# A GNN convolution kernel: edge-range work of VectorE in 18 parts, GpSimd's tables at the head, read-back tables at half step 10

## What is computed

```python
h   = x @ W_in + b_in
Wij = (ssp(edge_attr @ Wf1 + bf1) @ Wf2 + bf2) * edge_weight[:, None]   # ssp = softplus - log 2
agg = segment_sum(h[dst] * Wij, src)
x   = layernorm(x + ssp(agg @ Wo1 + bo1) @ Wo2 + bo2)
# graph attention over the same edges:
e     = leaky_relu(h_att[src] @ a1 + h_att[dst] @ a2); e -= max(e)
alpha = exp(e) / (segment_sum(exp(e), dst)[dst] + 1e-9)
x   = layernorm(x + leaky_relu(x + neigh + (x * neigh) @ W2 + b2))
#   neigh = segment_sum((x @ W1 + b1)[src] * alpha, dst)
```

## Time and profile before

| | before |
|---|---|
| median of 3 runs | 1405.86 us (1402.91 to 1408.44) |
| the profiled execution, its own time | 1404.69 us |
| its span, first to last instruction | 1402.6 us |
| busy: PE, VectorE (DVE), ScalarE (ACT), GpSimd (POOL) | 83%, 86%, 61%, 59% |
| mean granted TensorE clock | 0.919 of full speed |

### The profile page before, as it was taken

One profiled execution on the slowest core, in us unless ns is written; L12 is line 12 of the kernel. 1 busy time (PEld: TensorE's weight loads), 2 busy tenths in 40 slices (PEclk: granted clock), 3 DMA queues, 4 the chain that ended last, 5 costly groups with the idle time before them and its releaser, 6 DMA issues. The chain is left out here.

```text
span 1402.6 us, 27868 instructions
## 1 busy us (share of the span) xinstructions
PE 1162.7 (83%) x8987; PEld 946.7 (67%) x9079; DVE 1204.6 (86%) x2226; ACT 853.5 (61%) x2125; POOL 831.4 (59%) x909
## 2 busy tenths in 40 slices
PE   4778767688899968899888999999999495777895
PEld 4444445357778756788767877777777384777895
DVE  8798866549899968799889999999998279999986
ACT  1456664478788978688888888888875044000023
POOL 5167777777777777777777777777777330000011
PEclk8688887899999999999999999999999798879998
DMA  7233342258899568899699999989897773776661
GB/s 263 68 81 91 89 115 79 74 124 215 222 263 255 190 194 225 240 251 258 179 244 263 242 244 260 264 230 241 246 265 203 178 245 104 241 226 222 230 226 37
DMA packets 246738, 276.49 MB, mean 197 GB/s; under 512 B 35121, under 2 KB 194511, under 8 KB 243252
## 3 DMA queue, kind: packets, MB, share of 16 engines
q1 hardware_dynamic: 200128, 185.24, 45.5%
q0 software_dynamic: 25856, 53.42, 12.2%
q10 hardware_dynamic: 20596, 35.89, 12.0%
HBM read 163.26 MB, written 111.20 MB: 196 GB/s over the span
## 5 line engine op out<-in xcount | busy, mean ns | idle before, releaser
L1929 POOL DMA_INDIRECT edge_rows<-x_rows,pos x808 | 783.5, 970 | 286.6 <-issue 225.8
L1441 ACT ACTIVATE h_edge<-ps_wh,w_col 128x128 f32<-128x128 f32 x808 | 229.4, 367 | 112.1 <-PE ps_wh L1232 99.7
L1276 PEld LDWEIGHTS ps_d<-back_one,back 128*128 128x128 f32 x1914 | 231.2, 192 | 59.4 <-issue 56.0
L1276 PE MATMUL ps_d<-back_one,back 128*128 128x128 f32 x1914 | 240.3, 278 | 4.3 <-DVE agg_t L1743 4.0
L1239 PE MATMUL ps_wh<-wf,filt 128*128 128x128 f32 x1616 | 237.5, 293 | 1.5 <-DVE filt L1545 1.4
L1225 PE MATMUL ps_v<-f_t,wf 128*128 128x512 f32 x400 | 223.1, 641 | 0.0
L1549 DVE TENSOR_TENSOR x_rows<-ps_wh,h_edge 128x512 f32<-128x512 f32 x202 | 138.0, 683 | 85.0 <-ACT h_edge L1441 37.9
L1239 PEld LDWEIGHTS ps_wh<-wf,filt 128*128 128x128 f32 x1616 | 208.0, 201 | 3.4 <-DVE filt L1545 3.4
L1065 PE MATMUL ps_wh<-yard 128*128 128x150 bf16 x1575 | 139.1, 234 | 59.7 <-DVE yard L1055 29.7
L2393 PE MATMUL ps_wh<-loan,yard 128*126 128x129 f32 x1250 | 155.2, 288 | 38.9 <-DVE yard L2643 30.8
L1065 PEld LDWEIGHTS ps_wh<-yard 128*128 128x128 bf16 x1575 | 110.0, 100 | 103.7 <-DVE yard L1055 73.1
(11 more groups left out here) (346 smaller groups left out, 1398.8 us busy)
## 6 DMA issues: line engine op xcount, KB each, us to landing
c_tab<-yard SPq DMA_DIRECT2D x25, 1575.0 KB
yard<-c_tab SPq DMA_DIRECT2D x25, 1575.0 KB, 6.6
dst_bc<-dst ACTq DMA_DIRECT2D x99, 252.0 KB
back<-edge_rows SPq DMA_DIRECT2D x42, 516.0 KB, 8.5
edge_rows<-x_rows,pos POOLq DMA_INDIRECT x808
back<-edge_rows SPq DMA_DIRECT2D x48, 258.0 KB, 5.0
m_tab<-yard SPq DMA_DIRECT2D x25, 393.8 KB
mask_room<-m_tab SPq DMA_DIRECT2D x5, 1968.8 KB, 12.4
```

Of the source, the lines that this page charges most:

```text
L1276: mm = nc.tensor.matmul(acc(c), back_rows(n)[:, k0 + t, 0:D], back_one[:, m % 2, o + t, :], start=t == 0, stop=t == k1 - k0 - 1, skip_grou ...
L1441: copy = nc.scalar.activation(h_edge[:, j, q, :], ps_wh[:, bank, 1, q * D:(q + 1) * D], ACT.Copy, scale=w_col[:, t(q)])
L1929: return pool.indirect_dma_start(table[s], bass.IndirectOffsetOnAxis(places_here, 0), rows, None)
```

## The change

It does three things. VectorE's edge ranges go from 9 parts to 18, one at each half step from 24 to 41, with TensorE's five parts at 28, 30, 33, 36 and 38; the operations are the same, some in another order, and the fourteen comparisons go in four parts of 4, 3, 4 and 3, the seven `picks` in parts of 2, 3 and 2. All that follows (pairs, counts) begins one half step later. GpSimd makes its constant tables before its first scatter, without waiting for anything, in the buffer `back_one`, which nobody uses before half step 50; one of the seven tables is dropped for an existing one (`ones3`). `rest_of_tables` moves from half step 4 to half step 10, where it stands behind the pieces of that half step.

```diff
-CS_HIGH, CS_LOW, CS_RUN, CS_UNDER, CS_BELOW, CS_PASSES = 9, 10, 11, 13, 14, 19
+CS_HIGH, CS_RUN, CS_UNDER, CS_BELOW, CS_PASSES = 8, 11, 16, 19, 25
...
+            tables = back_one[:, 0, :, :].rearrange("p k n -> p (k n)")
+            anti = tables[:, 0:P]
+            blk_i = tables[:, P:P + NK].bitcast(I32)
...
+            TABLES_AT = 10
             R_FROM = 24
-            P_FROM = R_FROM + 16
+            P_FROM = R_FROM + 17
...
+            RANGE_STEPS = 18
             def ranges_dve_at(k):
-                return {R_FROM: 0, R_FROM + 5: 1, R_FROM + 6: 2, R_FROM + 7: 3, R_FROM + 8: 4, R_FROM + 9: 5,
-                        R_FROM + 11: 6, R_FROM + 13: 7, R_FROM + 15: 8}.get(k)
+                return k - R_FROM if R_FROM <= k < R_FROM + RANGE_STEPS else None
             def ranges_pe_at(k):
-                return {R_FROM + 7: 0, R_FROM + 9: 1, R_FROM + 10: 2, R_FROM + 12: 3, R_FROM + 14: 4}.get(k)
+                return {R_FROM + 4: 0, R_FROM + 6: 1, R_FROM + 9: 2, R_FROM + 12: 3, R_FROM + 14: 4}.get(k)
...
+                    if r == 6:
+                        link(nc.vector.tensor_scalar(src7, work_i[:, 2, :, :], 255, 8, ALU.bitwise_and,
+                                                     ALU.logical_shift_left))
+                        dve.wait_ge(r7_made, 6)
                         nc.vector.tensor_copy(iota_lo, iota_f[:])
                         nc.vector.tensor_copy(iota_key, key_i)
                         nc.vector.tensor_copy(tid, tid_i)
                         nc.vector.tensor_copy(three, three_i)
-                        nc.vector.tensor_scalar(blk_first, blk_i, float(W), None, ALU.mult)
-                        nc.vector.tensor_scalar(blk_last, blk_i, float(W), float(W - 1), ALU.mult, ALU.add)
-                        nc.vector.tensor_scalar(blk_key, blk_i, 256.0, None, ALU.mult)
-                        nc.vector.tensor_scalar(work_i[:, 0, :, :], src7, 7, None, ALU.logical_shift_right)
...
-                        for c in range(SC):
-                            nc.vector.tensor_scalar(under[:, 0, c, :], blk_first, high_col[:, c:c + 1], None, ALU.is_gt)
-                            ins = nc.vector.tensor_scalar(under[:, 1, c, :], blk_last, low_col[:, c:c + 1], None, ALU.is_ge)
-                        link(ins)
+                        under_parts(0, 0, 4)
+                    if r == 11:
+                        link(under_parts(0, 4, SC))
...
+                    if r == 12:
+                        nc.vector.tensor_scalar(blk_key, blk_i, 256.0, None, ALU.mult)
+                        under_parts(1, 0, 4)
...
+                    if r == 17:
+                        picks(5, SC).then_inc(pick_done, 1)
...
-                        if k == 4:
+                        if k == TABLES_AT:
                             rest_of_tables()
...
                 def range_tables():
-                    pool.wait_ge(pos_put, NRB)
-                    pool.wait_ge(h_end_out, 16)
                     nc.gpsimd.memset(anti, 0.0).then_inc(r7_made, 1)
...
                         for k in range(2 * GS[s], 2 * GS[s + 1]):
-                            if k == R_FROM:
-                                range_tables()
...
+                range_tables()
                 with pool.If(n_win > 1):
                     more_windows()
```

More of the change, by code:

```diff
@@ L864, in build @@
             wide_one = back_one[:, :, :, :].rearrange("p u k n -> p (u k) n")
+            tables = back_one[:, 0, :, :].rearrange("p k n -> p (k n)")
+            anti = tables[:, 0:P]
+            blk_i = tables[:, P:P + NK].bitcast(I32)
+            tid_i = tables[:, P + NK:P + NK + SC].bitcast(I32)
+            key_i = tables[:, P + NK + SC:P + NK + SC + KW].bitcast(I32)
+            three_i = tables[0:1, P + NK + SC + KW:P + NK + SC + KW + MAXP].bitcast(I32)
+            assert P + NK + SC + KW + MAXP <= QT_LATE * P
             abs_done = sem("abs_done")
@@ L1020, in pair_products, with picks @@
                 mm.then_inc(done, 1)
-            def picks():
-                for c in range(SC):
+            def picks(c0=0, c1=SC):
+                for c in range(c0, c1):
                     ins = nc.vector.tensor_scalar(pick[:, c, :], tile_of[:, :, :].rearrange("p b k -> p (b k)"),
@@ L1282, in ranges_part @@
                     if r == 0:
-                        pe.wait_ge(r7_made, 7)
+                        pe.wait_ge(r7_made, 6)
                         pe.wait_ge(cs, 2)
@@ L1304, in ranges_part @@
                             for c in range(SC):
-                                mm = nc.tensor.matmul(ps_d[:, b, 0:n], ones_bf, under[:, r - 3, c, s:s + n], start=c == 0,
+                                mm = nc.tensor.matmul(ps_d[:, b, 0:n], ones3[:], under[:, r - 3, c, s:s + n], start=c == 0,
                                                       stop=c == SC - 1)
@@ L1636, in ranges_part, with under_parts @@
                 def ranges_part(r):
+                    def under_parts(u, c0, c1):
+                        edge, at, op = ((blk_first, high_col, ALU.is_gt), (blk_last, low_col, ALU.is_ge))[u]
+                        for c in range(c0, c1):
+                            ins = nc.vector.tensor_scalar(under[:, u, c, :], edge, at[:, c:c + 1], None, op)
+                        return ins
                     if r == 0:
@@ L1649, in ranges_part @@
                         nc.vector.tensor_copy(three, three_i)
-                        nc.vector.tensor_scalar(blk_first, blk_i, float(W), None, ALU.mult)
-                        nc.vector.tensor_scalar(blk_last, blk_i, float(W), float(W - 1), ALU.mult, ALU.add)
-                        nc.vector.tensor_scalar(blk_key, blk_i, 256.0, None, ALU.mult)
-                        nc.vector.tensor_scalar(work_i[:, 0, :, :], src7, 7, None, ALU.logical_shift_right)
[L1654 to L1675, removed]
+                    if r == 7:
                         dve.wait_ge(ranges_mm, 2)
@@ L1679, in ranges_part @@
                         nc.vector.tensor_tensor_scan(high_run, high_row, high_row, 0.0, ALU.max, ALU.max)
+                    if r == 8:
                         link(nc.vector.tensor_tensor_scan(low_run, low_row, low_row, float(PAD_DST), ALU.min, ALU.min))
                         assert ranged[0] == CS_RUN
-                    if r == 6:
+                        link(nc.vector.tensor_scalar(dst7, work_i[:, 2, :, :], 8, 16, ALU.logical_shift_right,
+                                                     ALU.logical_shift_left))
+                    if r == 9:
+                        nc.vector.tensor_copy(key_part[:, 1, :, :], src7)
+                        link(nc.vector.tensor_copy(key_part[:, 2, :, :], dst7))
+                        link(nc.vector.tensor_scalar(blk_first, blk_i, float(W), None, ALU.mult))
+                    if r == 10:
                         dve.wait_ge(ranges_mm, 3)
@@ L1685, in ranges_part @@
                         link(nc.vector.tensor_copy(low_col, ps_d[:, 0, SC:2 * SC]))
-                        for c in range(SC):
-                            nc.vector.tensor_scalar(under[:, 0, c, :], blk_first, high_col[:, c:c + 1], None, ALU.is_gt)
-                            ins = nc.vector.tensor_scalar(under[:, 1, c, :], blk_last, low_col[:, c:c + 1], None, ALU.is_ge)
-                        link(ins)
+                        under_parts(0, 0, 4)
+                    if r == 11:
+                        link(under_parts(0, 4, SC))
                         assert ranged[0] == CS_UNDER
-                    if r == 7:
+                        link(nc.vector.tensor_scalar(blk_last, blk_i, float(W), float(W - 1), ALU.mult, ALU.add))
+                    if r == 12:
+                        nc.vector.tensor_scalar(blk_key, blk_i, 256.0, None, ALU.mult)
+                        under_parts(1, 0, 4)
+                    if r == 13:
                         dve.wait_ge(ranges_mm, 4)
@@ L1696, in ranges_part @@
                         link(ins)
+                        link(under_parts(1, 4, SC))
                         assert ranged[0] == CS_BELOW
-                    if r == 8:
+                    if r == 14:
+                        for k in range(KT):
+                            ins = nc.vector.tensor_scalar(tile_of[:, :, k], below, float(k), None, ALU.add)
+                        link(ins)
+                    if r == 15:
                         dve.wait_ge(ranges_mm, 5)
-                        for k in range(KT):
-                            nc.vector.tensor_scalar(tile_of[:, :, k], below, float(k), None, ALU.add)
                         for b, n in ((0, NK // 2 + 1), (1, NK // 2)):
@@ L1707, in ranges_part @@
                         link(nc.vector.tensor_reduce(span_top, spans, AX, ALU.max))
+                        picks(0, 2)
+                    if r == 16:
                         link(nc.vector.tensor_scalar(more, three, span_top[0:1, 0:1], None, ALU.is_lt))
@@ L1711, in ranges_part @@
                         assert ranged[0] == CS_PASSES
```

(6 more changed lines are left out.)

28 lines of the change are left out of this document (18 added, 10 removed).

## The result

The changed kernel takes 1401.26 us (median of 20 runs, 1396.98 to 1405.89) where the kernel before takes 1405.17 (20 runs beside it): a ratio of 0.9975, 95% interval 0.9966 to 0.9984. By the ratio that is 3.5 us, by the medians 3.9; the two can differ by 0.1%, in the experiments too. The gain is under the bound of 0.5%, but clear of noise. The profiled execution of the changed kernel took 1402.75, its span 1400.7; the one of before 1404.69 and 1402.6. So the two traces differ by 1.9 us only, one of each.

What follows compares the result with a forecast made beforehand. GpSimd's chain of 808 scatters was taken as the bound. Tables -1.8, head +0.9 and ranges -2.2 gave -3.1 us, so the median was to go from 1405.86 to 1402.8; range 1397.0 to 1407.5.

Steps and rivals of the forecast that it cites:

- the head: Up to scatter 14: it starts 0.9 us later than before, from the tables' collision and the moved read-back tables.
- signs of being wrong: Scatter 14 well before 138, the ranges' excess under 2 or over 7 us, or a gap growing at half step 189.
- GpSimd bounds the kernel: From the first scatter to the node stage, only shortening GpSimd's scatter chain or ending its gaps shows in the time.
- GpSimd's tables, -1.8: At half step 24: making the tables before scatter 0 and dropping the seventh gains 1.8 us.
- The collision at the head, +1.0: Before product 0: tables beside VectorE's first operations cost between 0 and 2.0 us; the middle, 1.0, was taken.
- Read-back tables at 10, 0: Half steps 4 to 14: gaps at 5 and 7 return at 11 and 14; 0 taken, ends +0.6 and -1.2 us.
- 18 parts, -2.2: VectorE's ranges: splitting long rows makes their 9.0 us cost scatters 2.3 instead of 4.5, at 0.25 a microsecond.
- The gain arrives whole: Behind the ranges producers still wait for GpSimd, so the gain passes whole, with 0.3 to 0.5 us of doubt.
- Rival D: At half step 189: producers hold GpSimd and what was won is waited there; 1405.6 us, chance 0.06.
- Rival A: In the ranges: blocks vanish, excess falls from 7.2 to 1 or 2, head loses nothing; 1398.3 to 1397.1, chance 0.20.
- B: In the ranges: every VectorE operation blocks by itself, parts don't matter, excess stays at 7.2; 1405.0 us, chance 0.18.
- C: In the ranges: every part meets a scatter at the long row's rate, excess rises to 15.4; 1413.2 us, chance 0.06.

Runs made afterwards that it cites:

- e9: The changed kernel measured once more, unaltered, beside three later runs: 1400.78 against 1405.78 us for the kernel before, ratio 0.9960.
- e11: e10 with a semaphore increment and wait behind each of the fourteen comparisons, the three tile_of operations and blk_key: 1395.21 against 1405.78 us, ratio 0.9919.
- e10: Changed kernel with read-back tables at half step 21 and both scans reading one input from the accumulation memory: 1396.99 against 1405.78 us, ratio 0.9939.
- e7: Changed kernel with both range scans reading one input from the accumulation memory, each right behind its row's copies: 1397.51 against 1406.44 us, ratio 0.9937.
- e6: Changed kernel with the read-back tables at half step 21 instead of 10: 1398.18 against 1406.44 us for the kernel before, ratio 0.9938.
- e2: Changed kernel with GpSimd's tables made at half step 24 again: 1403.18 against 1406.90 us for the kernel before, ratio 0.9981.
- e1: Changed kernel with only its 18 parts left, GpSimd's tables at half step 24 and read-back tables at 4 again: 1403.78 against 1406.90 us, ratio 0.9988.
- e4: Kernel before, in its 9 parts, with a semaphore increment and wait behind each fast operation of parts 1 and 6: 1403.81 against 1406.90 us, ratio 0.9986.
- e12: Kernel before with its read-back tables at half step 21 instead of 4, nothing else: 1402.84 against 1405.78 us, ratio 0.9984.
- e3: Changed kernel with the read-back tables at half step 4 again: 1404.30 against 1406.90 us for the kernel before, ratio 0.9983.
- e5: Changed kernel with the count groups spread until half step 196 instead of 190: 1402.59 against 1406.44 us for the kernel before, ratio 0.9978.
- e8: Changed kernel with the edits of e5, e6 and e7 together: 1399.82 against 1406.44 us for the kernel before, ratio 0.9950.

## Why the prediction was right, and where not

Forecast were 3.1 us less, 1402.8; measured is 1401.26, 3.5 less by the ratio, inside the range. That the sum came so near is in part luck. By the two traces, in the changed kernel scatter 14 starts 1.3 us earlier where 0.9 later was forecast, the tables give 1.7, the ranges 1.4, and 1.8 are lost behind half step 42: the head was priced too high by 2.2 us and the loss at the end at almost nothing, and the two nearly cancel. Two of the signs of being wrong came: scatter 14 before 138 (137.27, in e9 135.96), and a gap that grows at 189. Item by item:

**GpSimd bounds the kernel: right.** From scatter 42 to 201 every trace takes 804.5 to 806.9 us, 159 half steps of 5.05 being 803, so a gain made before 42 arrives but for the gaps at the end. The four kernels with the shortest times (e11, e10, e7, e6) are among the seven with the shortest way from scatter 0 to 201; single traces don't order them further.

**GpSimd's tables, -1.8: right.** From scatter 14 to 24 it took 52.4 us, in the changed kernel 50.8; e2 brings 1.7 back.

**The collision at the head, +1.0: too large.** The step took the middle between 0 and the tables' length, with a copy of 4.02 us as its row. VectorE's first operations in the changed kernel:

```profile
56.62 0.58 DVE L1892 TENSOR_SCALAR yard<-src_col 128x808 int32<-128x808 int32 x1 [2.64 <-PEq L401]
57.23 0.58 DVE L1894 CAST lo_f<-yard 128x808 f32<-128x808 int32 x1
57.73 0.70 DVE L1543 TENSOR_SCALAR onehot_t<-dst_bc,base_p,win_off 126x512 bf16<-126x512 int16 x1
```

Two are not lengthened and the third takes 0.70 where it took 0.41. GpSimd's iota of 525 columns became longer too: it took 0.97, and 0.56 before. From VectorE's first operation of the block to scatter 0 it takes 7.65 to 7.66 us in the traces without the tables there (before, e1, e2, e4, e12) and 7.94 to 7.96 in those with them that have this row (changed, e3, e5, e6, e8 to e11): the price is 0.3. The rule of the Trainium skill (SBUF — State Buffer, "SBUF: two separate sides"), whichever starts first holds the other off for one instruction, gave some tenths; here the trace agrees, with 0.29 on one VectorE operation.

**Read-back tables at 10, 0: right where it can be compared.** The gaps went to 11 and 14, VectorE's 5.9 us coming back in front of product 11. At the lower clock of the head they are 3.1 (e2) and 3.7 (e7) together, where those at 5 and 7 were 3.0 in the kernel before; at the higher clock they are 1.3 to 1.5. So of the 2.2 us by which the head was mis-sized 0.7 is the collision, and the other 1.5 goes with a clock that the prediction didn't ask about and that the change, as far as the traces show, doesn't set. What I also didn't ask is where the tables would cost less: at 21 the products are 2 to 9 us ahead of GpSimd from half step 11 to 21, once the tables aren't in front of them. With them there scatter 14 comes about 3 us sooner after scatter 0 than with the tables at 4 (e6, e8, e10, e11, e12), and at the lower clock 1.5 to 1.9 of it is lost again at 22.

**18 parts, -2.2: right in size, half in reason.** By the two traces of the changed kernel the excess fell by 1.4 and 2.9. In the seven traces with the 18 parts and the old scans (changed, e1, e2, e3, e5, e6, e9) it is 4.6 to 6.3, in the two with the 9 parts (before, e12) 7.7 and 9.2. That an unbroken row of VectorE blocks as one was the reason given, and e4 shows it, though not every scatter beside a row was held to its end (see the last section). That the short rows would cost 0.25 a microsecond was not the right form: in the kernel before the scatters beside the two scans already took 1.68 and 1.61, half of the 2.7 that it spread over all the rest, and in the changed kernel the two scans alone cost 3.0 of the 6.3 left, and nothing with another input (e7).

**The gain arrives whole: not quite.** Rival D had 0.06 and was partly there: the gap at 189 grew by 1.3 us in one trace and by 0.2 in the other. e2 shows that it isn't a fixed time the producers hold, for with everything 1 us later it stayed 1.6; e5 shows that it moves when work is moved. What decides between 0.5 and 1.6 in the same kernel stays open; the clock of the head doesn't, since both values occur in both groups.

Rival A's path is what e10 and e11 took, by other edits; B is refuted by e4 for the rows, C by the excess of the changed kernel.

## What to carry to other kernels

Find the engine whose chain has no gaps, even if it is the least busy one, and price every item on it: its gaps, its side work, and instructions that last longer than their usual time. Side work of an engine that feeds it belongs where the feed is furthest ahead, and moving a lump from one tight place to the next only moves the gap. Before a gap is put down to an edit, set the granted clock of its stretch beside that of the other trace: here the same code had a gap of 0.8 or of 3.1 us. Where VectorE runs rows of one-source SBUF operations or operations with two SBUF inputs beside GpSimd's indirect DMAs, break the rows with a wait or read one input from the accumulation memory. The waits make VectorE's work longer, and where it is all in one half step that can cost most of the gain again (e4).

## What the runs showed of the hardware

- A scatter can be held by a row of one-source VectorE operations without gaps until the end of the whole row: it ended 0.13 us after the tenth operation and, at the other row, 0.13 us after the fourteenth; in e12 it was 0.12 us at both. The Trainium skill's page SBUF — State Buffer, in "A bandwidth-pool intuition that's wrong (but worth ruling out)", gives the end of the VectorE operation plus about 115 ns: the trace agrees on the delay, but what had to end for the long scatters is the row, where the page speaks of one operation.
- Not every scatter beside such a row is held that long: one that started 1.3 us into the row of fourteen got through in 1.30 us, with the row still running, and one in e12 did so in 1.29. Why isn't known. GpSimd's timeline of the kernel before:

```profile
243.98 1.30 POOL L1929 DMA_INDIRECT edge_rows<-x_rows,pos  x1 [0.30 <-issue]
```

- A wait with its gap of 0.03 us behind each operation is enough to let scatters in (e4).
- A scan of 2.0 us on one partition with both inputs in SBUF lengthened scatters by 1.81 and 1.15 us; with one input in the accumulation memory, and a wait on both sides, by nothing, at the same length (e7). Two such scans in a row didn't act as one: in e4 a scatter of 1.74 us that started in the first ended 0.77 us after it, while the second was running.
- Comparisons that start 0.41 us apart in a row start 0.63 us apart on average with a wait behind each (e4, with scatters running beside them).
